# An attention and routed-expert kernel on one core: the row maxima of the scores taken for both heads at once, their columns carried by DMA, and all projections row-tiled

## What is computed

```python
xn = layernorm(x)
h = layernorm(xn) * ln_scale + ln_bias
c_q, c_kv = h @ w_down_q.T, h @ w_down_kv.T          # 128 wide
q, k, v = c_q @ w_up_q.T, c_kv @ w_up_k.T, c_kv @ w_up_v.T   # 16 heads of 64
q, k = rope(q), rope(k)
attn = softmax((q @ k.T) / 8)                         # per head, 1024 x 1024
s = (attn @ v) @ w_out.T + xn
g = silu(routed_experts(xn) + xn)                     # 2 of 8 experts a token
out = x + s * g
```

## Time and profile before

| | before |
|---|---|
| median of 3 runs | 3657.75 us (3653.6 to 3657.8) |
| profiled execution: own time, span | 3655.32 us, 3653.8 us |
| PE, busy share of the span | 99% |
| PE weight loads | 65% |
| DVE | 87% |
| ACT | 76% |
| POOL | 33% |
| DMA, mean share in most of the attention | 0.6 to 0.7 |
| granted clock of PE | 0.998 |

### The profile page before, as it was taken

One profiled execution on the slowest core, in us unless ns is written; L12 is line 12 of the kernel. 1 busy time (PEld: TensorE's weight loads), 2 busy tenths in 40 slices (PEclk: granted clock), 3 DMA queues, 4 the chain that ended last, 5 costly groups with the idle time before them and its releaser, 6 DMA issues. The chain is left out here.

```text
span 3653.8 us, 77190 instructions
## 1 busy us (share of the span) xinstructions
PE 3599.4 (99%) x24217; PEld 2364.0 (65%) x24217; DVE 3195.1 (87%) x4341; ACT 2759.1 (76%) x4016; POOL 1199.8 (33%) x1178
## 2 busy tenths in 40 slices
PE   7999999999999999999999999999999999999999
PEld 5754554545544554545554555454699999999999
DVE  8889999999999999999999999999777777777799
ACT  5778888888878888888888888888766666666665
POOL 2212222222222222222222222232366666666400
PEclk9999999999999999999999999999999999999999
DMA  7985767676666666666667676765666666666798
GB/s 257 358 283 142 185 156 186 157 185 161 180 160 176 170 174 169 171 171 166 177 165 181 160 186 156 184 162 136 193 222 215 217 223 216 214 224 216 235 369 274
DMA packets 378436, 724.74 MB, mean 198 GB/s; under 512 B 105277, under 2 KB 253886, under 8 KB 342272
## 3 DMA queue, kind: packets, MB, share of 16 engines
q0 software_dynamic: 83504, 340.66, 36.2%
q1 hardware_dynamic: 294864, 383.23, 31.8%
HBM read 453.60 MB, written 138.81 MB: 162 GB/s over the span
## 5 line engine op out<-in xcount | busy, mean ns | idle before, releaser
L1180 ACT ACTIVATE at_ex<-at_st 128x1024 f32<-128x1024 f32 x1024 | 1048.8, 1025 | 138.3 <-PE at_st L1327 132.8
L1383 PE MATMUL at_pv<-at_ex,at_v 128*64 128x512 f32 x4096 | 991.6, 605 | 0.0
L1037 DVE TENSOR_REDUCE at_mx<-at_fr 128x1 fp32r<-128x512 f32 x1024 | 705.9, 689 | 202.5 <-PE at_fr L1393 169.6
L1204 ACT ACTIVATE at_fr<-at_fr 128x512 f32<-128x512 f32 x1024 | 603.4, 589 | 243.0 <-PE at_fr L1393 229.7
L1383 PEld LDWEIGHTS at_pv<-at_ex,at_v 128*64 128x64 f32 x4096 | 248.3, 136 | 471.1 <-issue 462.2
L1050 DVE TENSOR_TENSOR at_sum<-at_sum,at_ex 128x1024 f32<-128x1024 f32 x448 | 545.3, 1217 | 3.7 <-ACT at_ex L1180 3.4
L1393 PE MATMUL at_fr<-at_kfar,at_qh 64*128 64x512 f32 x1024 | 459.7, 449 | 5.9 <-DVE at_mx L1037 4.5
L1390 PE MATMUL at_fr<-at_kdif,at_qh 64*128 64x512 f32 x1024 | 461.4, 451 | 1.8 <-DVE at_mx L1037 0.9
L1327 PE MATMUL at_st<-at_qh,at_kh 64*128 64x512 f32 x2048 | 452.8, 392 | 3.8 <-DMA at_top<-at_mneg 3.7
L1390 PEld LDWEIGHTS at_fr<-at_kdif,at_qh 64*128 64x128 f32 x1024 | 187.7, 183 | 413.7 <-issue 356.9
L1327 PE MATMUL at_st<-at_ql,at_kh 64*128 64x512 f32 x2048 | 452.0, 391 | 0.0
(11 more groups left out here) (213 smaller groups left out, 6359.4 us busy)
## 6 DMA issues: line engine op xcount, KB each, us to landing
at_cq<-scr_c SPq DMA_DIRECT2D x62, 1024.0 KB, 6.1
at_ck<-scr_c SPq DMA_DIRECT2D x62, 1024.0 KB, 5.2
at_sum<-at_sum POOLq DMA_DIRECT2D x95, 512.0 KB, 6.0
scr_v<-pj_v SPq DMA_DIRECT2D x64, 512.0 KB, 6.8
at_v<-scr_v SPq DMA_DIRECT2D x64, 512.0 KB, 6.6
mid_rec<-scr_rec SPq DMA_DIRECT2D x256, 128.0 KB, 5.1
scr_o<-mid_oT SPq DMA_DIRECT2D x64, 512.0 KB, 3.0
at_rotq<-at_swpq POOLq DMA_DIRECT2D x126, 256.0 KB, 4.6
```

The costliest lines, as they stand in the source:

```text
L1037: e.reduce_max(mx[k // QB][:, h * QB + k % QB:h * QB + k % QB + 1], fr[h][:, :], AX.X).then_inc(s_tr[h], 1)
L1180: e.activation(ex[k][:, :, :], st[u % 2][:, :, :], ACT.Exp, scale=SCALE).then_inc(s_exp, 1)
L1204: e.activation(fr[h][:, :], fr[h][:, :], ACT.Relu).then_inc(s_pos[h], 1)
L1383: mm = e.matmul(pv[n][rows[h], :], v[i.u][:, kt, rows[h]], ex[kt][:, h, :], start=(kt == 0), stop=(kt == KT - 1))
```

## The change

Eight things change.

- Both heads of a slot go together: x is `differ` of both, ACT's relu takes 128x1024, y is `add` of both, and DVE's maximum takes 128x2x512 and writes two columns. `fr` is one tile of two banks.
- `turn_maxima`, `negate`, `mneg` and the identity are gone. For each slot, as soon as its maximum is there, SP issues two DMAs, each of one column of `mx` (128 partitions, 4 bytes each) into a row of `top`. The sign is in `one_row`, which now holds -1.
- All projections are row-tiled: keys in steps 2 and 3, queries in steps 6 and 7.
- ACT's order: relu, exponential 2g, a copy in some steps, exponential 2g+1, further copies. `far_keys` is done for `two` in step 7, before its second exponential; it was done for `one` in step 1. `high` of the keys moves from step 2 to step 4.
- DVE's order: one maximum in a step. `turn_cos` of the keys moves to the end of step 4 and `turn_sin` ahead of the maximum of step 5; `low` of the queries moves from step 1 to 2.
- SP: the broadcast of reciprocals is split: `gather` to DRAM at the end of the turn, and `each` in the next turn, between column DMAs.
- The first pair's columns go by the same DMAs, all six ahead of its load of values.
- Waits on banks name other semaphores to match.

```diff
-        fr = [ps(f"fr{h}", [P, HALF]) for h in range(2)]
+        fr = ps("fr", [P, 2, HALF])
...
-            def max_rows(j, n):
-                e.wait_ge(s_neg, j.n(2, n + 1))
+            def max_rows(j, k):
+
+                wait_apart(e, s_tr, j.n(NSLOT_Q, k + 1), s_apart_s)
                 for h in range(2):
-                    r = rows[h].start
-                    e.dma_start(top[j.u][r:r + 1, bank[n]].bitcast(F32).rearrange("o (t q) -> o t q", q=P),
-                                mneg[n][h * QB:(h + 1) * QB, :].bitcast(F32)).then_inc(s_mrow[n], 16)
+                    r, col = rows[h].start, h * QB + k % QB
+                    e.dma_start(top[j.u][r:r + 1, k * P:(k + 1) * P].bitcast(F32), mx[k // QB][:, col:col + 1].bitcast(F32),
+                                allow_slow_non_contiguous=True).then_inc(s_mrow[k // QB], 16)
...
-            def broadcast(i, halves, k=0):
+            def gather(i, halves, k=0):
                 e.wait_ge(s_recc, i.n(1, k + 1))
                 for n in halves:
                     e.dma_start(scr["rec"][i.n(), n:4:2, :].rearrange("h (p k) -> p h k", p=P), recc[:, :, n, :]).then_inc(s_recd, 16)
+
+            def each(i, n):
+
+                e.wait_ge(s_recd, i.n(32, 32))
+                for h in range(2):
+                    e.dma_start(rec[n][rows[h], :], scr["rec"][i.n(), 2 * h + n, :].unsqueeze(0).broadcast_to((DH, HALF))).then_inc(s_rec[n], 16)
...
+                one = i.next(1)
+                older = prev and not (isinstance(i.n(), int) and i.n() < 2)
                 if ahead >= 3:
                     load(i.next(3), Q)
+                max_rows(i, 6)
+                if older:
+                    each(prev.next(-1), 0)
+                max_rows(i, 7)
+                if older:
+                    each(prev.next(-1), 1)
                 if ahead:
-                    load_v(i.next(1))
-                max_rows(i, 1)
+                    load_v(one)
+                    max_rows(one, 0)
                 if ahead >= 3:
                     load(i.next(3), K)
+                if ahead:
+                    max_rows(one, 1)
+                    max_rows(one, 2)
                 if prev:
                     spread(prev, (0, 1))
                 if ahead:
-                    max_rows(i.next(1), 0)
+                    for k in (3, 4, 5):
+                        max_rows(one, k)
...
-            def maximum(j, k, h, ready):
-
-                if k % QB == 0 and h == 0:
-                    wait(e, s_tf, j.n(2, k // QB - 1))
-                e.wait_ge(ready, j.n(NSLOT_Q, k + 2 - (h == 0)))
-                e.reduce_max(mx[k // QB][:, h * QB + k % QB:h * QB + k % QB + 1], fr[h][:, :], AX.X).then_inc(s_tr[h], 1)
+            def maximum(j, k):
+
+                if k % QB == 0:
+                    wait(e, s_mrow[k // QB], j.n(32 * QB))
+                e.wait_ge(s_y, j.n(NSLOT_Q, k + 1))
+                e.reduce_max(mx[k // QB][:, k % QB:2 * QB:QB], fr[:, :, :], AX.X).then_inc(s_tr, 1)
...
                     if g == 5 and most:
-                        turn_cos(two, K)
+                        turn_sin(two, K)
...
                     if g < 2 or more:
-                        maximum(*slot_of(i, g), 0, s_y)
+                        maximum(*slot_of(i, g))
                     for added in late:
                         add_keys(*added)
-                    if g == 1 and more:
+                    if g == 2 and more:
                         low(one, Q)
                     if g == 3 and most:
                         turn_sin(two, Q)
                     if g == 4 and older:
                         normalise(prev.next(-1), 0)
-                    if g == 5 and most:
-                        turn_sin(two, K)
+                    if g == 4 and most:
+                        turn_cos(two, K)
                     if g == 7 and prev:
                         recip(prev)
                     if g == 7 and older:
...
-            def gain(j, k, h, ready):
-
-                e.wait_ge(ready, j.n(NSLOT_Q, k + 1))
-                e.activation(fr[h][:, :], fr[h][:, :], ACT.Relu).then_inc(s_pos[h], 1)
+            def gain(j, k):
+
+                e.wait_ge(s_x, j.n(NSLOT_Q, k + 1))
+                e.activation(fr[:, :, :], fr[:, :, :], ACT.Relu).then_inc(s_pos, 1)
...
+                    if g < 2 or more:
+                        gain(*slot_of(i, g))
+                    exps(i, 2 * g)
+                    if g == 1 and prev:
+                        out_copy(prev, 1)
+                    if g == 2 and ahead >= 2:
+                        proj_copy(two, K, 0, pv[1])
                     if g == 5:
                         out_copy(i, 0)
-                    if g < 2 or more:
-                        gain(*slot_of(i, g), 0, s_x)
-                    if g == 0 and prev and ahead >= 2:
-                        proj_copy(two, Q, 1, pv[0])
-                    if g == 4 and ahead >= 2:
-                        proj_copy(two, K, 1, pv[1])
-                    exps(i, 2 * g)
-                    if g < 2 or more:
-                        gain(*slot_of(i, g), 1, s_y)
+                    if g == 6 and ahead >= 3:
+                        proj_copy(three, Q, 0, pv[0])
+                    if g == 7 and ahead >= 2:
+                        far_keys(two)
                     exps(i, 2 * g + 1)
                     if g == 4 and prev:
                         den_copy(prev, 1)
-                    if g == 1 and ahead >= 2:
-                        proj_copy(two, K, 0, pv[1])
-                    if g == 2:
-                        negate(i, 1)
-                    if g == 5 and ahead >= 3:
-                        proj_copy(three, Q, 0, pv[0])
-                    if g == 6 and more:
-                        negate(one, 0)
+                    if g == 4 and more:
+                        high(one, K)
+                    if g == 3 and ahead >= 2:
+                        proj_copy(two, K, 1, pv[1])
+                    if g == 7 and ahead >= 3:
+                        proj_copy(three, Q, 1, pv[0])
                     if g == 0 and more:
                         high(one, Q)
-                    if g == 1 and more:
+                    if g == 1 and more and not prev:
                         far_keys(one)
-                    if g == 2 and more:
-                        high(one, K)
...
-                    e.wait_ge(s_mrow[u // KT], i.n(32, 32))
+                    e.wait_ge(s_mrow[u // KT], i.n(32 * QB, 32 * QB))
...
+            def upper_rows(i, u, j, x, n, dst):
+
+                if n == 0:
+                    e.wait_ge(s_ld[x][j.u], j.same(32, 32))
                 scores_free(i, u)
                 for k in range(3):
-                    mm = project_row(j, x, k, 0, dst)
+                    mm = project_row(j, x, n, k, 0, dst)
...
+            def step_x(j, k):
+
+                if k == 0:
+                    e.wait_ge(s_fold, j.n(1, 1))
+                    e.wait_ge(s_hi[Q], j.n(1, 1))
+                wait(e, s_tr, j.n(NSLOT_Q, k))
+                differ(j, k, 0)
+                differ(j, k, 1).then_inc(s_x, 1)
 
             def step_y(j, k):
 
                 if k == 0:
                     e.wait_ge(s_far, j.n(1, 1))
-                e.wait_ge(s_pos[0], j.n(NSLOT_Q, k + 1))
-                wait(e, s_tr[1], j.n(NSLOT_Q, k))
+                e.wait_ge(s_pos, j.n(NSLOT_Q, k + 1))
                 add(j, k, 0)
-                differ(j, k, 1).then_inc(s_y, 1)
-
-            def turn_maxima(j, n):
-                for h in range(2):
-                    e.wait_ge(s_tr[h], j.n(NSLOT_Q, QB * (n + 1)))
-                e.matmul(pv[n][0:2 * QB, 0:P], mx[n][:, :], ident_r[:, :], start=True, stop=True).then_inc(s_tf, 1)
+                add(j, k, 1).then_inc(s_y, 1)
...
+                    if g == 2 and ahead >= 2:
                         if prev:
                             e.wait_ge(s_osb, i.n(2, 0))
                         else:
                             e.wait_ge(s_raw[Q], 6)
+                        return two, K, 0, pv[1]
+                    if g == 3 and ahead >= 2:
+                        e.wait_ge(s_raw[K], two.n(2, 1))
+                        return two, K, 1, pv[1]
+                    if g == 6 and ahead >= 3:
+                        e.wait_ge(s_osb, i.n(2, 1))
+                        return three, Q, 0, pv[0]
+                    if g == 7 and ahead >= 3:
+                        e.wait_ge(s_raw[Q], three.n(2, 1))
+                        return three, Q, 1, pv[0]
...
                     now = slot_of(i, g) if g < 2 or ahead else None
-                    before = (slot_of(i, g - 1) if g else (i, 5)) if g < 3 or ahead else None
-                    if now or before:
-                        step_x(now, before)
+                    if now:
+                        step_x(*now)
```

123 lines of the change are left out of this document (32 added, 91 removed).

## The result

The changed kernel takes 3604.95 us, the median of four runs (3603.57 to 3606.97), against 3657.78 (3653.6 to 3658.27) for the kernel before, measured beside it on the same chip: a ratio of 0.9858, 95% interval 0.9841 to 0.9876, or 53 us less. The prediction was 3614, within 3602 to 3652. The profiled execution took 3603.57 us, its span 3602.0, against 3655.3 and 3653.8 before. One of the ten executions of relu_late, further down, took 8782 us and stands for nothing here: its other nine lie within 5.2 us of each other.

A forecast was written before the change was run, and what follows sets the result against it. PE was taken to set the pace, busy all 36.88 us of a turn. Savings of 50.0 us, less 5 for the first pairs and 2 for lateness near loads, left 43 off 3657.75: 3614 us, range 3602 to 3652.

The forecast's parts named there:

- PE's terms: Savings on PE from shape changes, transposes and step 1's late y: 0.80 us a turn, 50.0 us in all.
- the transposes: PE's 128 transposes of maxima go, 0.15 us each: 19.2 us saved.
- the shape changes: PE's switches between 64-row and 128-row products go in 123 projection halves, 0.21 us each: 25.8 us saved.
- the late y of step 1: In step 1 y's weights wait for relu, delaying the next product 0.08 us; gone in 62 turns: 5.0 us saved.
- The first pairs: Before scores begin, the longer chain is not hidden and values load later: 5 us of loss, between 0 and 10.
- Late turns near a load: Small lateness in the turns near a load: 2 us of loss.
- The loop x, relu, y, maximum: One chain for both heads: relu 1.00 to 1.03 us, y at x + 1.72, maximum 1.22 us; no loss taken.
- y late: Rival: relu ends after y's weight load is due in six steps; with a late maximum 3622 to 3651, chance 0.20.
- kfar: ACT's copy in step 7 finds the keys' DMA landed, no wait; rival up to 3726 us, chance 0.09.
- SP: Sixteen column issues at 0.60 us plus about 10.5 for the rest: 20 of 36 us a turn, no loss.
- the rival's threshold: SP becomes the bound from 1.6 us a column; at 2.0, about 4005 us; chance 0.07 with other DMA holds.
- Pairing costs nothing: On PE, putting both heads' x together and y together costs nothing, as two 64-row products stood side by side before.

The follow-up runs named there:

- relu_late: The changed kernel with a 64-column copy on ACT between the wait for x and relu: 3653.57 us, ratio to before 0.9995.
- before_with_columns: The kernel before with the maxima sent as column DMAs, without transposes, negations and row DMAs, and with the broadcasts split: 3633.59 us, ratio 0.9941.
- full_rows: The changed kernel with the first halves of keys and queries again on 128 rows, not row-tiled: 3624.8 us, ratio to before 0.9912.
- columns_twice: The changed kernel with each column also sent to the row below, 32 column DMAs a turn: 3731.98 us, ratio to before 1.0204.
- broadcast_same_turn: The changed kernel with the reciprocals' broadcasts behind their gather in the same turn, as before: 3640.43 us, ratio to before 0.9951.
- half_step_free: The changed kernel with heads half a step apart, keys' turn_cos starting step 5 and turn_sin behind head 1's maximum in step 6: 3603.04 us, ratio to before 0.9859.
- half_step: The changed kernel with heads half a step apart again, relu and maximum for each head, DVE's order as changed: 3645.34 us, ratio to before 0.997.

## Why the prediction was right

It said 43 us less and 53 came.

The mechanism is right: PE sets the pace before and after, its own work shrank by the terms of the sum, and no engine beside it took the gain back. (The last step of the sum, 3614.75, rounds to 3615, not 3614.)

*PE's terms* were 0.80 us a turn, 50.0 in all. By the table the median steps sum to 36.88 before and 36.09 after: 0.79. Of it, the transposes are 0.34 (0.30 forecast: one costs 0.17 rather than the 0.15 between starts), the shape changes 0.39 of step length and 0.35 of turn (0.42 forecast), the late y of step 1 the difference of the two full-row steps in before_with_columns, 4.92 - 4.81 = 0.11 (0.08 forecast). The errors of sizing cancel, which is luck; the mechanism of each is shown, by before_with_columns and full_rows for two of them. That y's delay is gone with relu's new place shows only in the changed kernel's own step 1; no run took it apart.

*The first pairs* were set at 5 us of loss. The first product with a row of maxima stands at 241.256 us before and at 242.345 after: 1.1 us. This is 4 of the 10 us by which the forecast was short, in part by luck: the chain's first x stands at 218.28 us before and at 217.13 after, so the stage ahead of it ended 1.15 us earlier in the execution after, and the chain itself lost 2.2 us.

*Late turns near a load* were set at 2 us of loss; they gained instead. The six long turns, 3.1 us, were in the trace of before, and the prediction had no term for them. With the 2 us that is 5, and with the first pairs 9 of the 10 us.

*The loop x, relu, y, maximum.* x to y 1.71 to 1.74 (1.72 forecast), relu and maximum as forecast. So is the weight load of y, 0.1 us late in six of eight steps, at x + 1.60; one of the signs, that it would not idle on ACT, contradicts this. "About the edge" holds: these loads idle 0.13 to 0.15 us at no cost, relu_late's 0.30, and that costs 0.14. The rival *y late*, 3651 at 0.1 us a step, was one short copy away; relu_late lands on it, at 3653.6.

*DVE.* In step 5 the maximum was to start at x5 + 2.4; it starts at 1030.88, which is 1028.46 + 2.42, right behind `turn_sin`, and x6 comes in time:

```profile
1029.74 1.22 DVE L1027 TENSOR_TENSOR at_swpk<-at_rawk,at_sin 128x1024 f32<-128x1024 f32 x1
1030.88 1.22 DVE L1059 TENSOR_REDUCE at_mx<-at_fr 128x2 fp32r<-128x1024 f32 x1
```

*kfar.* POOL was to begin at x5 + 3.0 and ACT to come at x5 + 11.4; the rows say 3.07 and 11.46, without idling of ACT:

```profile
1031.53 1.72 POOL L960 DMA_DIRECT2D at_rotk<-at_swpk  x2 [2.01 <-DVE at_swpk L1027]
```

```profile
1039.92 0.62 ACT L1216 ACTIVATE at_kfar<-at_rotk 128x512 fp32r<-128x512 f32 x1
```

*SP.* 20 of 36 us were forecast and 0.62 x 36.08 = 22 measured: the median issue was right and the mean, 0.69, is what adds up. What failed here is the rival's threshold. It put SP's bound at 1.6 us a column, that is 25.6 us of columns in a turn; 32 columns at 0.69 are 22 and already bind. What the sum lacked is the small instructions and the gaps between issues, 6 us a turn in columns_twice: 22 and the forecast's 10.5 for the rest would have fitted into 36.08; with these 6 they do not. It also took the broadcasts' new place for one with ample cover, without saying that with columns the old one has none: broadcast_same_turn prices that place at 35 us.

*Pairing costs nothing*: shown by half_step_free. That it gains nothing either, and that half_step's first answer was DVE's queue, the prediction did not say.

Left open: what makes a column's issue last up to 1.6 us at times, how much of half_step's step 5 is ACT's `high` and how much DVE's order, and what made the six turns of the kernel before long.

## What to carry to other kernels

When an experiment that undoes one edit answers with the rival's number, look at which step grew and what stands ahead of the late instruction in its own queue: here 40 us looked like the worth of pairing and were gone once the keys' rotation stood elsewhere in DVE's order. A wait that an in-order queue reaches too early holds all that stands behind it, and costs as much as that is due: the same 2.6 us a turn were nearly free before, and 35 us in all once columns stood behind them. Moving it to where its event is long past was worth more than either edit on PE (22 to 24 us in before_with_columns, 20 in full_rows). And a slack of hundredths of a microsecond, six times a turn, is worth measuring by a small deliberate delay, since the next edit may use it up.
